# Second attention of a two-layer Flamingo block: frequency-major spectra, inverse transform per tile, all rolls first, residuals on TensorE

## What is computed

```python
x = x + tanh(g_xattn[0]) * softmax_attention_with_rope(layernorm(x), ctx)      # 16 heads of 8
x = x + tanh(g_ffn[0])   * top2_of_8_experts(layernorm(x))                     # 512 hidden
x = x + tanh(g_xattn[1]) * autocorrelation_attention(layernorm(x), ctx)        # the part changed
x = x + tanh(g_ffn[1])   * fp4_mlp(layernorm(x))                               # 352 hidden

# autocorrelation_attention, for each sequence and head of 8 features
Q, K, V = x @ Wq + bq, ctx @ Wk + bk, ctx @ Wv + bv
corr = irfft(rfft(Q) * conj(rfft(K))).mean(over the 8 features)                # 64 lags
w, idx = top_k(corr, 4); w = softmax(w)
out = sum_k w[k] * V[(t + idx[k]) % 64]                                        # a circular roll
return out @ Wo + bo

# fp4_mlp: inputs, hidden values and weights are rounded to 4-bit floats in blocks of 16,
# each scaled by its largest magnitude / 6;  h = silu(gate) * up;  h @ w_down
```

## Time and profile before

| | |
|---|---|
| median of 3 runs | 277.76 us (274.62 to 280.14) |
| profiled execution | 274.7 us, span 272.9 us |
| busy: PE, DVE, ACT, POOL | 251.0, 191.9, 165.3, 131.3 us |
| granted TensorE clock, mean | 0.994 of full speed |
| HBM read, written | 9.71 MB, 1.05 MB |

### The profile page before, as it was taken

One profiled execution on the slowest core, in us unless ns is written; L12 is line 12 of the kernel. 1 busy time (PEld: TensorE's weight loads), 2 busy tenths in 40 slices (PEclk: granted clock), 3 DMA queues, 4 the chain that ended last, 5 costly groups with the idle time before them and its releaser, 6 DMA issues.

```text
span 272.9 us, 6251 instructions
## 1 busy us (share of the span) xinstructions
PE 251.0 (92%) x2152; PEld 195.1 (72%) x2152; DVE 191.9 (70%) x494; ACT 165.3 (61%) x384; POOL 131.3 (48%) x207
## 2 busy tenths in 40 slices
PE   8999999999798989999999999979998774999886
PEld 6655367777577869999999999664884442666675
DVE  3898588888998764442222223885769989999993
ACT  2369986666488556675666667463545793254553
POOL 4475579999602404209992220374156634253230
PEclk9999999999999999999999999999999999799999
DMA  6999000000000209877677770000000000000111
GB/s 194 376 345 410 19 4 2 2 4 2 0 2 4 80 19 374 346 291 292 270 294 291 310 298 14 2 1 1 4 0 0 0 0 2 0 19 23 38 40 38
DMA packets 12191, 30.11 MB, mean 110 GB/s; under 512 B 1024, under 2 KB 5248, under 8 KB 12032
## 3 DMA queue, kind: packets, MB, share of 16 engines
q1 hardware_dynamic: 12160, 29.71, 28.8%
HBM read 9.71 MB, written 1.05 MB: 39 GB/s over the span
## 4 chain that ended last, share of the span: by engine, by line
PE 61%; DVE 22%; issue 7%; ACT 5%; POOL 2%; SPq 1%; DMA 1%; DVEq 0%; POOLq 0%
PE ps L1414 12%; PE ps L1403 11%; PE ps L1252 5%; DVE s_region L294 5%; PE ps L1226 5%; PE ps L1239 4%; PE ps L1159 3%; DVE s_region L1090 3%; PE ps L1542 3%; PE ps L1150 3%; DVE s_small L1095 2%; PE ps L1151 2%; PE ps L1262 2%; DVE s_small L237 2%; DVE s_region L286 1%
## 5 line engine op out<-in xcount | busy, mean ns | idle before, releaser
L631 ACT ACTIVATE s_region<-ps,s_region 128x128 f32<-128x128 f32 x144 | 41.1, 370 | 22.0 <-PE ps L1403 22.0
L960 DVE SCALAR_TENSOR_TENSOR s_ctxT<-ps,s_region,s_ctxT 128x64 f32 x72 | 18.1, 282 | 44.3 <-PE ps L1414 44.3
L1403 PE MATMUL ps<-s_region 128*128 128x128 f32 x288 | 38.2, 276 | 0.5 <-issue 0.3
L1414 PE MATMUL ps<-s_region 128*128 128x128 f32 x288 | 37.9, 275 | 0.0
L1403 PEld LDWEIGHTS ps<-s_region 128*128 128x128 f32 x288 | 34.9, 192 | 1.1 <-issue 0.7
L1414 PEld LDWEIGHTS ps<-s_region 128*128 128x128 f32 x288 | 35.0, 192 | 0.2 <-issue 0.2
L420 POOL COPY s_region<-s_xt 128x64 f32 x72 | 14.8, 237 | 31.0 <-PE ps L1403 23.2
L1599 PE MATMUL ps<-s_region 128*128 128x352 f32 x64 | 21.9, 484 | 5.0 <-DVE s_region L1090 3.3
L574 ACT COPY s_region<-ps 128x512 f32<-128x512 f32 x32 | 17.2, 593 | 15.1 <-PE ps L1239 15.1
L1252 PEld LDWEIGHTS ps<-s_region 128*64 128x64 f32 x512 | 16.3, 138 | 12.9 <-ACT s_region L574 11.1
L830 DVE TENSOR_REDUCE s_small<-ps 128x16 f32<-128x1024 f32 x16 | 19.6, 1225 | 8.0 <-PE ps L1226 7.9
(11 more groups left out here) (230 smaller groups left out, 524.9 us busy)
## 6 DMA issues: line engine op xcount, KB each, us to landing
s_region<-s_wall SPq DMA_DIRECT2D x36, 514.0 KB, 3.0
s_wall<-wall SPq DMA_DIRECT2D x8, 514.0 KB, 9.3
s_par<-par SPq DMA_DIRECT2D x1, 1280.0 KB, 10.6
s_x<-x SPq DMA_DIRECT2D x2, 512.0 KB, 6.9
out<-s_x SPq DMA_DIRECT2D x6, 128.0 KB, 1.8
s_region<-ffn SPq DMA_DIRECT2D x1, 560.0 KB, 3.6
s_ctxT<-ctxT SPq DMA_DIRECT2D x2, 256.0 KB, 4.1
s_ctxT<-ctxT SPq DMA_DIRECT2D x1, 512.0 KB, 6.8
```

Of the source, the lines that this page charges most:

```text
L631: ins = act.activation(hg[j % 3][:, c, :], ps[:, j % 3, RPT * S * c:RPT * S * (c + 1)], ACT.Gelu, bias=wbuf[j % 6][:, FF + FC * D + c:FF + ...
L960: dve.scalar_tensor_tensor(row, ps[:, 4 + j % 2, S * k:S * k + S], w, row, ALU.mult, ALU.add).then_inc(m["acc_done"], 1)
L1403: ins = mm(ps[:, j % 3, RPT * S * c:RPT * S * (c + 1)], w[:, P * c:P * c + P], xg[j % 4], start=True, stop=True)
L1414: ins = mm(ps[:, 4 + j % 2, 0:RPT * S], w[:, FF + D * c:FF + D * c + D], hg[j % 3][:, c, :], start=(c == 0), stop=(c == FC - 1))
```

## The change

A float32 product is two passes on TensorE in the trace, a transpose one.

- Spectra are made frequency-major. `spectrum` runs twice (once for each half) with two 128x128 products, in place of eight times with two 128x256. ScalarE's four broadcast copies become two plain ones (`weights_by_lag`). VectorE repeats each number for its 8 features while it reads PSUM.
- Values are made frequency-major too: four 128x128 products for each group and no bias. The bias of the values goes through Wo instead: `bias_product` in the first attention gets two more products, which make `bo1g`, and GpSimd one more copy (`bvrep1`). `bo1g` is scaled there and no longer at the end of the experts.
- The swapped half is no longer added on GpSimd. `to_time` transforms each tile back with two products that accumulate, one with `idft_o` and one with `idft_x`, the same table with its halves swapped, which four small transfers bring in behind the loads of `wall`. Then `out_tokens` multiplies with Wo, four 128x128 products for each group.
- All four groups add `x` on TensorE (`residual`), take statistics from PSUM and are copied back by ScalarE. The gate is applied in `y1_turned`.
- VectorE does all eight rolls ahead of the first statistics. Tiles 6 and 7 are normalised by VectorE, no longer ScalarE. GpSimd unscales group 0 ahead of the third power. Weights are turned inside `to_time`'s sequence.

```diff
-SPEC_BANK = (0, 1, 6, 7)
-OUT_BANK = (5, 1, 7, 6)
+LAG_BANK = (0, 4)
+TURN_BANK = (4, 2)
+TIME_BANK = (2, 3, 2, 3)
+WEIGHT_BANK = (0, 4, 2)
+OUT_BANK = (1, 5, 7, 6)
...
+            lo, hi = COL["idft_o"]
+            for u in range(2):
+                for c in range(2):
+                    r, q = 2 * DFT * u + DFT * c, 2 * DFT * u + DFT * (1 - c)
+                    sp.dma_start(idft_x[r:r + DFT, :], a["par"][q:q + DFT, lo:hi]).then_inc(m["ld_back"], 16)
...
+                pool.tensor_copy(bvrep1, pc("bias1")[:, 2:3].broadcast_to([P, P])).then_inc(m["bias_rows"], 1)
...
-            values_added(0)
+            pool.wait_ge(m["g_done"], 1)
             for z in [xb] + hb:
                 pool.memset(z[:, :, BLK:], 6e-12).then_inc(m["floors_set"], 1)
-            for q in range(1, 6):
-                values_added(q)
             powers(pool, 0, 4)
-            values_added(6)
-            values_added(7)
             powers(pool, 4, 8)
+            x_unscale(0)
             powers(pool, 8, 12)
-            x_unscale(0)
+            x_unscale(1)
             powers(pool, 12, 16)
-            x_unscale(1)
...
+            sum_kept(0)
+            act.wait_ge(m["x3_done"], 1)
             normalise(act, 0, 4, m["xn_d"], 11, blocked=True)
             y1_turned(2)
+            sum_kept(1)
+            act.wait_ge(m["x3_done"], 2)
+            normalise(act, 4, 6, m["xn_d"], 12, blocked=True)
             x_magnitude(0)
             y1_turned(3)
-            normalise(act, 4, 8, m["xn_d"], 12, blocked=True)
-            sum_kept(2)
...
+            def roll_values(r):
+
+                g, z = r // 2, r % 2
+                half, odd = g // 2, g % 2
+                dve.wait_ge(m["kv_used"], G4 + g + 1)
+                dve.wait_ge(m["g_done"], half + 1)
+                lags = ps[:, LAG_BANK[half], P * z:P * z + P].rearrange("p (k g h) -> p k g h", k=4, g=2)[:, :, odd, :]
+                out, v = (y[:, 4 * g:4 * g + 4, :].rearrange("p t (h d) -> p t h d", d=HD) for y in (of[:, z], vf))
+                dve.tensor_tensor(out, lags.unsqueeze(3).broadcast_to([P, 4, H, HD]), v, ALU.mult).then_inc(m["of_done"], 1)
...
-            attention_out(0)
-            roll_values(6)
-            roll_values(7)
-            attention_out(1)
+            sum_stats(0)
+            sum_stats(1)
             x_scale(0)
-            sum_stats(2)
+            dve.wait_ge(m["x3_done"], 2)
+            normalise(dve, 6, 8, m["xn_d_dve"], 12, blocked=True)
             x_round(0)
             x_scale(1)
+            sum_stats(2)
+            x_round(1)
             sum_stats(3)
-            x_round(1)
...
+            def to_time(g, first=0, last=4):
+
+                pe.wait_ge(m["of_done"], 2 * g + 2)
...
+                for k in range(first, last):
+                    out = ps[:, TIME_BANK[g], P * k:P * k + P]
+                    mm(out, of[:, 0, 4 * g + k, :], pc("idft_o"), start=True, stop=False)
+                    ins = mm(out, of[:, 1, 4 * g + k, :], idft_x, start=False, stop=True)
...
+            def residual(g):
+
+                pe.wait_ge(m["bo_added"], g + 1)
...
+                mm(ps[:, OUT_BANK[g], :], ident, x[:, 4 * g:4 * g + 4, :].rearrange("p t d -> p (t d)"), start=True, stop=False)
+
+            def out_tokens(g):
+
+                pe.wait_ge(m["y1_ready"], g + 1)
                 for k in range(4):
+                    ins = mm(ps[:, OUT_BANK[g], P * k:P * k + P], y1[g % 2][:, k, :], pc("wo1"), start=False, stop=(k == 3))
+                ins.then_inc(m["o_done"], 1)
...
             turn_lags(0)
             context_kv(7)
             spectrum(0)
+            residual(0)
+            turn_lags(1)
+            residual(1)
             spectrum(1)
...
+            to_time(0)
+            to_time(1, 0, 2)
             out_tokens(0)
+            to_time(1, 2, 4)
+            to_time(2, 0, 2)
             out_tokens(1)
+            to_time(2, 2, 4)
             turn_weights(0)
             turn_weights(1)
+            to_time(3)
+            residual(2)
             turn_weights(2)
+            out_tokens(2)
+            residual(3)
+            out_tokens(3)
```

More of the change, by code:

```diff
@@ L1042, in _ @@
             best_lags(1)
-            for q in range(6):
+            for q in range(8):
                 roll_values(q)
             dd = Steps(dve, m["dve_d"])
-            def attention_out(g):
-                dve.wait_ge(m["bo_added"], g + 1)
-                dve.wait_ge(m["o_done"], g + 1)
-                dve.scalar_tensor_tensor(group(x, g), ps[:, OUT_BANK[g], :], tg[:, 2:3], group(x, g), ALU.mult, ALU.add).then_inc(m["x3_done"], 1)
-                dve.wait_ge(m["x3_done"], g + 1)
-                ln_stats(dve, dd, 4 * g, 4 * g + 4)
             def sum_stats(g):
@@ L1067, in x_scale @@
                 u = g % 2
-                dve.wait_ge(m["xn_d"], 4 * g + 4)
+                dve.wait_ge(m["xn_d"], 4 * g + (2 if g else 4))
+                if g == 1:
+                    dve.wait_ge(m["xn_d_dve"], 2)
                 if g >= 2:
@@ L1247, in weigh_values @@
                 else:
-                    pe.wait_ge(*((m["bias_ready"], 1) if t else (m["q_raw"], 4)))
+                    pe.wait_ge(*((m["bo_scaled"], 1) if t else (m["q_raw"], 4)))
                 n = 2 * (HD + 1)
@@ L1343, in context_kv @@
                 lo = 512 * (n % G4)
-                mm(ps[:, bank, P * first:P * last], pc("wk1" if n < G4 else "wv1"), ctxF[:, lo + P * first:lo + P * last], start=True, stop=False)
-                ins = frequency_bias(bank, 1 + n // G4, slice(2 * first, 2 * last))
+                if n < G4:
+                    mm(ps[:, bank, P * first:P * last], pc("wk1"), ctxF[:, lo + P * first:lo + P * last], start=True, stop=False)
+                    ins = frequency_bias(bank, 1, slice(2 * first, 2 * last))
+                else:
+                    for k in range(first, last):
+                        ins = mm(ps[:, bank, P * k:P * k + P], ctxF[:, lo + P * k:lo + P * k + P], pc("wv1"), start=True, stop=True)
                 if last == 4:
@@ new lines, in turn_lags, with spectrum @@
+                tr(ps[:, TURN_BANK[h], 0:P], gw.rearrange("p b s -> p (b s)"), ident).then_inc(m["lags_turned"], 1)
+            def spectrum(h):
+                pe.wait_ge(m["gt_ready"], h + 1)
+                pe.wait_ge(m["pp_done"], 2 * G4)
+                if h == 0:
+                    pe.wait_ge(m["rolled_made"], 2)
+                for z in range(2):
+                    ins = mm(ps[:, LAG_BANK[h], P * z:P * z + P], rolled[:, P * z:P * z + P], gT[h], start=True, stop=True)
+                ins.then_inc(m["g_done"], 1)
@@ new lines, in to_time @@
+            def to_time(g, first=0, last=4):
+                pe.wait_ge(m["of_done"], 2 * g + 2)
+                if g == 0:
+                    pe.wait_ge(m["gt_ready"], 2)
+                    pe.wait_ge(m["ld_back"], 64)
+                elif g == 1:
+                    pe.wait_ge(m["kv_used"], 2 * G4)
+                else:
+                    pe.wait_ge(m["y1_ready"], g - 1)
+                for k in range(first, last):
+                    out = ps[:, TIME_BANK[g], P * k:P * k + P]
+                    mm(out, of[:, 0, 4 * g + k, :], pc("idft_o"), start=True, stop=False)
+                    ins = mm(out, of[:, 1, 4 * g + k, :], idft_x, start=False, stop=True)
+                if last == 4:
+                    ins.then_inc(m["y1_done"], 1)
```

122 lines of the change are left out of this document (35 added, 87 removed).

## The result

| | before | after |
|---|---|---|
| median us (lowest to highest, runs) | 274.93 (274.12 to 280.14, 20) | 271.94 (271.23 to 275.52, 20) |
| ratio after to before | | 0.9873, 95% interval 0.9848 to 0.9898 |
| profiled execution, span | 272.9 | 270.1 |
| mean granted clock of TensorE | 0.994 | 0.994 |

The change makes the kernel 1.3% faster by this ratio, and 2.99 us or 1.1% by the medians: less than two per cent, with an interval clear of no change. The 20 runs of the kernel before put its median at 274.93, at the level of its profiled execution, and not at the 277.76 of the three runs shown earlier. The spans differ by 2.8 us.

A forecast was written before the change was run, and what follows sets the result against it. VectorE was taken to bound the kernel from hh(0) on; 2.3 + 0.8 = 3.1 us off 274.7 gave 271.6, off the shown median 274.7, and the middle, 273.1 us, was forecast. Range 269.3 to 277.2.

The forecast's parts named there:

- the profiled level: Whole kernel: the changed median sits like the profiled run, 274.7 less 3.1, giving 271.6 us.
- I take the middle: Whole kernel: 273.1 us, between 271.6 from the profiled run and 274.7 from the shown median of 277.76.
- hh(0) to the end counts one for one: From the last MLP's first product on, time is VectorE's; hh(0)'s gain reaches the end unless another engine becomes late.
- x_scale(0), 2.3 us: End of the second attention: the first FP4 scale on VectorE starts at 206.15 us, not 208.43.
- the slower rival of 1.22 us rolls: VectorE's rolls ahead of the statistics take up to 1.22 us each, making the kernel 0.8 us slower, 275.5; 7%.
- x_scale(0) to hh(0), 0.8 us: First FP4 scale to the last MLP's first product: 10.0 us, not 10.77.
- The avoided collision: VectorE's second shrinking step touches GpSimd's unscale by less than 0.1 us, taking 0.69 us, not 1.40; saves 0.7 us.
- The second rival: TensorE at 1.2 GHz on gate(0) and up(0), 5 us instead of 2.65; gain only 1.3, 273.4 us; 8%.
- silu(1): ScalarE, behind the last normalised tiles: ends at 220.6 us, wanted at 221.0; slack shrinks from 1.7 to 0.4 us.
- the first rival: ScalarE and GpSimd take over: silu(1) ends at 221.7, hh(1) loses 0.7 us; gain 2.4, 272.3 us; 15%.
- More than drawn: Later MLP pair steps: two shrinks freed of GpSimd collisions, 1.4 us more, gain 4.5, 270.2 us; 15%.
- Outside the stretch: Edits elsewhere, such as the second attention's bias products, are covered by waits; without that cover, 0.45 us at most.

The follow-up runs named there:

- Experiment 5: The changed kernel with groups 0 and 1 added to x by VectorE again, without their residual products on TensorE; x_scale(0) and hh(0) both 0.60 us later.
- experiment 6: The changed kernel with the last two rolls behind the statistics of group 0 on VectorE; x_scale(0) 12.47 and hh(0) 22.95 us behind the lags.
- experiment 1: The changed kernel with the last group's epsilon added by GpSimd ahead of its power, not by VectorE; one run, 271.04 us.
- experiment 2: The changed kernel with the MLP's first steps in the old order on VectorE and GpSimd; median 276.52 us, ratio to before 1.0096.
- Experiment 10: The changed kernel with the last group's epsilon on GpSimd, silu(1) ahead of the last normalised tiles, x's third group rounded behind the hidden layer's; 270.33 us, ratio 0.9824.
- the attention alone: The kernel of experiment 2 with four unread 512-column products added in TensorE's wait; ratio to before 1.0005, hh(0) 25.05 us behind the lags.
- the order alone: The kernel before with only the MLP's first steps in the new order; ratio to before 1.0011, hh(0) 25.80 us behind the lags.

## Why the prediction was right or wrong

- **The level.** Predicted 273.1, measured 271.94. The working on the profiled level gave 271.6, and the profiled execution took 271.89; the 1.5 us put on for the median of three runs were not needed. The step that missed is "I take the middle". That 271.6 came so close is in part luck: hh(0) came 2.40 us sooner and not 3.1, and 0.40 us ahead of the lags, for which the sum has no term, made up for more than half of the difference. The ends of the range, 269.3 and 277.2, are not worked out from the cases.
- **hh(0) to the end counts one for one.** Right: 53.70 in both.
- **x_scale(0), 2.3 us.** Measured 2.12 (14.58 less 12.46). Rolls have a pitch of 0.60 us as taken, so the slower rival of 1.22 us rolls is refuted. The first two groups' statistics start 7.78 and 10.61 us behind the lags, drawn 7.65 and 10.35: TensorE's bursts carry a tenth or two more than whole passes. The path is the one drawn: x_scale(0) waits for ScalarE's tiles of group 0 (0.35 us), and their chain starts with statistics 0, which wait for TensorE. Experiment 5 shows that 0.6 us of it come from the residuals on TensorE, experiment 6 that the rolls' place gives none. That the other 1.5 us come from the narrower spectra and the transform per tile is read from the timelines; no run takes these two apart.
- **x_scale(0) to hh(0), 0.8 us.** The term that was mis-sized: 10.49 us against 10.0 drawn and 10.77 before, so 0.28. The avoided collision is there, 0.69 instead of 1.40: the shrink starts at 210.97, the unscale ends at 211.06, and the touch of 0.09 us cost nothing. What the drawing left out is the next unscale: I let it end at 216.7 beside "statistics 3 end at 216.1" and asked only who waits for GpSimd, and not what VectorE runs beside it. It held the last step of those statistics for 0.64 us; experiment 1 shows it. The rest of that stretch was 0.15 us shorter than drawn.
- **TensorE.** gate(0) at 19.00 behind the lags (drawn 18.8), the granted clock 1.00 from 193 to 217: right. The second rival did not come, and experiment 2 shows how near it lay: with the new attention and the old order TensorE waits 3.22 us there, with the new order not at all.
- **silu(1).** Predicted slack 0.4 us. hh(1) does come without a wait, at 221.29, and silu(1) in the changed kernel leaves it more, 1.0 us:

```profile
219.57 0.73 ACT L721 ACTIVATE s_region<-ps 128x704 f32<-128x704 f32 x1
```

Experiment 1 uses that up from both sides, with hh(0) 0.84 us sooner and silu(1) 0.90 later, and VectorE waits. So the first rival is the next bound, not this one.
- **More than drawn.** The later collisions stayed as they were: 53.70 twice. Experiment 10 shows that one can be had, for 0.53 us.
- **Outside the stretch.** Taken as nothing; no difference above 0.1 us before 92 us. The 0.40 us that arise between there and 172 us I leave open.

The prediction's sum has two terms, 2.3 and 0.8 us, and they are not what the attention and the order are worth each. Those two do not add up: at full clock 0.3 us gained with the attention alone, 0.45 lost with the order alone, 2.4 gained together. The sum came near, 3.1 drawn for 2.40, because I walked the whole changed order and did not add edits.

## What to carry to other kernels

When a chain gets shorter, draw every engine's instructions through the same microseconds and look for pairs of VectorE and GpSimd that now overlap, small ones too: a four-element step can cost what a whole tile costs. An attention that ends sooner is worth little if TensorE then waits for a step that another engine has queued behind something else, and the wait can cost its clock as well. Time a two-part change in parts before deciding which part pays.

## What the runs showed of the hardware

- **A tiny instruction is held for a long one.** VectorE's four-element step took 0.81 us against 0.17 beside GpSimd's unscale, and GpSimd's small step 0.67 against 0.20 beside VectorE's shrink, so it works in both directions. GpSimd's power takes 1.04 us alone and 1.43 beside VectorE's round, whose instructions it does not lengthen. The Trainium skill, "SBUF — State Buffer", section "SBUF: two separate sides", calls the port pair that VectorE and GpSimd share an exclusive lock for a whole instruction. For the held steps and shrinks the trace agrees, and the 0.64 us on four elements are the price of being second. The power shows less than the rule says: it is 0.39 us longer, but the second instruction of the round runs beside it in its usual time (both take 1.43 us, alone 1.42).
- **What is not held.** hh(0) of experiment 1 started at 214.75, inside GpSimd's unscale (214.59 to 215.65), and took 0.85 us as alone. It has one operand in PSUM. The reductions and reciprocals behind hh(2) in experiment 10 keep their times too.
- **TensorE's clock after a wait.** After 3.22 us of idleness (experiment 2) it was granted 1.2 GHz until about 220.8 us; after the 1.61 us wait at 220.82 in the changed kernel it kept 2.4 GHz. After a wait of 2.64 us, at 228.95 in the changed kernel, it ran at 1.2 GHz too (0.50 from 229 to 231), at no cost, since VectorE does not wait for it there. The price in experiment 2 was 7.56 us for what takes 5.13 us.
